# A selective scan on one core: which engine multiplies by C, and a reordering of the small steps around it

## The chip, the cores and the metric

The program runs on one core of one Trainium2 chip. The core has five engines with an instruction queue each: TensorE (PE, with its weight loads PEld), VectorE (DVE), ScalarE (ACT), GpSimd (POOL) and SyncE (SP, which only issues transfers here). Every engine works through its queue in order, and waits on semaphores that others raise. Time is device microseconds (us) from the first to the last instruction. The kernel before took 2139.76 us, the median of three runs (2139.21 to 2142.21).

## The reference, cut to what matters

Sixteen sequences of 256 tokens and 128 features go through four Mamba blocks, a product with Wout, a layer norm, a mixture of eight experts and a second layer norm. One block is:

```python
xn = rmsnorm(x, norm_w)
xp, z = split(xn @ Win, 2)                        # 256 channels each
xc = silu(causal_conv4(xp, conv_w) + conv_b)
dt, Bm, Cm = split(xc @ Wx, [64, 80])             # 64 | 16 | 16
delta = softplus(dt @ Wdt + bdt)
for t in range(256):                              # per sequence, channel, state n of 16
    h = exp(delta[t] * A) * h + (delta[t] * xc[t]) * Bm[t]
    y[t] = sum_n h * Cm[t]
x = x + ((y + xc * Dp) * silu(z)) @ Wblk          # Dp: the skip
```

## The kernel before, in words

The 4096 tokens are eight groups of 512 (two whole sequences). A step is one group in one layer, so there are 32 steps; after them the experts run as a second phase, which the change does not touch. All engines run the same sequence of windows; window s holds the scan of step s, the end of step s-1 and the preparation of step s+1 (and the norm of s+2). Most windows stand in a hardware loop, two per turn.

A window has 16 slots. A slot scans two units of 32 channels x 4 states (128 partitions) over 512 tokens each, so its tile is 128 x 1024. Four slots in a row share an m (0 to 3), the state within a group of four. Per slot:

- **POOL and ACT** (`outer`, L469/L472 and L641) multiply delta * x, with tokens on partitions (`du_t`), by B into `dbu_t`: per m, 8 instructions on POOL and 8 on ACT, in one of two buffers. `POOL_SHARE` and `SHARE` say after which slots they stand, `POOL_FIRST` and `FIRST` the same for m = 0 of the next step.
- **ACT** (`exps`, L563) makes exp(delta * A) in one of four `decay` buffers.
- **PE** (`to_channels`, L1067) turns `dbu_t` by eight transposes into one of two PSUM tiles `dbu_ps`.
- **DVE** (`scan`, L829) runs the recurrence with `decay` (SBUF) and `dbu_ps` (PSUM) into one of eight `ring` tiles (SBUF; the profile's name for it, and for `dbu_t`, is `scan`).
- **DVE** for even slots (`times_c`, L838), **POOL** for odd ones (L478), multiply the ring tile by C (`c_rep`, SBUF) in place.
- **PE** (`quad`, L1052) sums two finished slots over the states into `y_ps`; this frees their ring tiles. DVE's `gate` (L844) multiplies `y_ps` by silu(z) after m = 3.

The preparation of the next step runs between the slots: conv and z projections on PE into the two banks `pre_ps`, Silu on ACT, `project_dbc`, a copy of dt, B and C to `dbc`, `project_dt`, softplus, then `delta`. Softplus is max(v,0) + log(1 + exp(-|v|)): ACT makes |v| (L600) and max(v,0) (L601) for each half, then Exp, Square and Ln; DVE corrects the logarithm in two instructions (L860, L864, both with two SBUF inputs) and adds (L868, `delta`). Sixteen DMAs copy delta to `d_rep` for the next step's exps. POOL forms delta * xc (`du`, L488, in the tile `sp_l`), PE transposes it (`turn_du`, L1145), ACT copies it out (`copy_dut`, L626), and only then can `outer` for m = 0 of the next step begin. `turn_b` and `copy_bt` bring B to token rows, `normalise` (POOL, L450) makes `xn`, `project_out` with `copy_out` ends the previous step, `skip` adds xc * Dp to `y_ps`.

## Time and profile before

| | |
|---|---|
| timed runs | 2139.21, 2139.76, 2142.21 us |
| the profiled execution | span 2143.5 us from first to last instruction; the page has no other time for it |
| before the first scan | 54.4 us |
| the 32 windows | from 54.4 us to 1708.8 us |
| experts | the last 435 us |
| busy share of the span | DVE 91%, PE 88%, ACT 79%, POOL 68% |

Engine shares are over the whole span; in the windows they differ, since POOL has almost nothing to do in the experts. Rows are read so: an engine, the kernel's line, the operation, output and inputs by the program's names, how often, the busy time, the mean duration of one, and the idle time in front with what ended it.

### The profile page before, as it was taken

The numbers are of one execution on the slowest core, as the hardware profiler recorded it, in microseconds if no ns is written. First come the engines' busy times: TensorE is split into PE (matmuls) and PEld (weight loads), VectorE is DVE, ScalarE is ACT, GpSimd is POOL, SyncE is SP. The second block draws the span as 40 slices with busy tenths as digits, with TensorE's granted clock in tenths as the row PEclk, the third lists the DMA queues.
The fourth block names the chain that finished last, engine by engine and source line by source line (L and its number), as shares of the span: only waits on it lengthen the run. The fifth ranks groups of instructions, "written<-read, shape, count | busy, mean of one in ns | idle before, by whom it ended". The sixth has DMA issues, their size and how long they took to land.

```text
span 2143.5 us, 34659 instructions
## 1 busy us (share of the span) xinstructions
PE 1877.8 (88%) x10816; PEld 1183.1 (55%) x10816; DVE 1943.2 (91%) x1826; ACT 1683.8 (79%) x3053; POOL 1458.1 (68%) x1364
## 2 busy tenths in 40 slices
PE   4788888888888888888888888888888799999998
PEld 1444444444444444444444445444444499989998
DVE  3799999999999999999999999999999987767775
ACT  4899999899999998989999999999999433333333
POOL 2688888888888888888888988888889600000000
PEclk9899999999999999999999999999999999999999
DMA  7323232323232323232333333332322200000000
GB/s 241 86 64 79 63 78 62 78 62 78 62 79 63 80 65 79 64 79 65 81 78 73 81 76 79 78 78 62 78 62 72 84 1 11 11 12 11 11 6 11
DMA packets 72786, 138.55 MB, mean 65 GB/s; under 512 B 13072, under 2 KB 31120, under 8 KB 68112
## 3 DMA queue, kind: packets, MB, share of 16 engines
q1 hardware_dynamic: 66320, 119.28, 22.7%
q10 hardware_dynamic: 6400, 18.42, 3.7%
q8 instruction: 39, 0.64, 0.1%
q14 instruction: 27, 0.22, 0.0%
HBM read 63.85 MB, written 7.74 MB: 33 GB/s over the span
## 4 chain that ended last, share of the span: by engine, by line
ACT 27%; PE 26%; POOL 26%; issue 13%; DVE 6%; ACTq 1%; SPq 1%; DMA 1%; POOLq 0%; DVEq 0%
POOL scan L478 12%; POOL scan L472 11%; PE y_ps L1291 11%; ACT decay L563 10%; PE dbu_ps L1266 8%; ACT scan L641 6%; DVE scan L829 3%; POOL scan L469 2%; PE dbu_ps L1067 2%; ACT sp_e L600 2%; ACT delta L601 2%; ACT sp_l L610 2%; PE y_ps L1052 2%; ACT sp_e L605 1%; ACT du_t L626 1%
## 5 line engine op out<-in xcount | busy, mean ns | idle before, releaser
L829 DVE TENSOR_TENSOR_SCAN scan<-decay,dbu_ps 128x1024 f32<-128x1024 f32 x512 | 1154.6, 2274 | 29.8 <-PE dbu_ps L1067 21.9
L1067 PE MATMUL dbu_ps<-ident,scan 128*128 128x128 f32 x4096 | 571.6, 286 | 220.7 <-DVE scan L829 195.9
L478 POOL TENSOR_TENSOR scan<-scan,c_rep 128x1024 f32<-128x1024 f32 x255 | 671.8, 2635 | 130.4 <-ACT du_t L626 66.5
L1067 PEld LDWEIGHTS dbu_ps<-ident,scan 128*128 128x128 f32 x4096 | 482.2, 147 | 500.1 <-DVE scan L829 259.3
L563 ACT ACTIVATE decay<-d_rep,a_cur 128x510 f32<-128x510 f32 x1024 | 668.0, 709 | 54.1 <-POOL scan L478 15.7
L472 POOL TENSOR_SCALAR scan<-du_t,b_t 128x256 f32<-128x256 f32 x896 | 594.8, 679 | 0.0
L641 ACT ACTIVATE scan<-du_t,b_t 128x256 f32<-128x256 f32 x1024 | 445.6, 494 | 1.2
L838 DVE TENSOR_TENSOR scan<-scan,c_rep 128x1024 f32<-128x1024 f32 x257 | 331.0, 1288 | 0.0
L766 ACT ACTIVATE decay<-dbu_ps 128x512 f32<-128x512 f32 x256 | 147.9, 597 | 205.2 <-PE dbu_ps L1266 183.1
L1052 PE MATMUL y_ps<-scan,sel 128*32 128x512 f32 x2048 | 299.8, 661 | 0.0
L1080 PE MATMUL pre_ps<-xn,w_pre 128*128 128x512 f32 x512 | 245.5, 603 | 5.2 <-DVE w_pre L818 5.2
L507 POOL TENSOR_TENSOR sp_e<-sp_e,bout_rep 128x512 f32<-128x512 f32 x8 | 11.2, 1399 | 277.1 <-DMA sp_e<-in_x_rows 277.1
L1266 PE MATMUL dbu_ps<-split_all 128*128 128x512 f32 x768 | 191.3, 400 | 5.8 <-DVE split_all L892 3.5
L1002 DVE TENSOR_TENSOR decay<-decay 128x512 f32<-128x512 f32 x256 | 163.6, 686 | 9.2 <-ACT decay L766 8.1
L1266 PEld LDWEIGHTS dbu_ps<-split_all 128*128 128x128 f32 x768 | 141.1, 190 | 35.2 <-issue 7.7
L989 DVE SCALAR_TENSOR_TENSOR xc<-y_ps,cw,xc 128x128 f32<-128x128 f32 x256 | 72.0, 344 | 95.4 <-PE y_ps L1291 95.4
L1080 PEld LDWEIGHTS pre_ps<-xn,w_pre 128*128 128x128 f32 x512 | 87.8, 191 | 97.4 <-issue 90.6
L488 POOL TENSOR_TENSOR sp_l<-delta,xc 128x1024 f32<-128x1024 f32 x32 | 75.2, 2351 | 81.2 <-DVE delta L868 81.2
L1291 PEld LDWEIGHTS y_ps<-w_pre,decay 128*128 128x128 f32 x1024 | 119.1, 192 | 3.6 <-issue 1.1
L1291 PE MATMUL y_ps<-w_pre,decay 128*128 128x128 f32 x1024 | 119.5, 275 | 0.2 <-DVE decay L1002 0.2
L1291 PEld LDWEIGHTS y_ps<-c_rep,decay 128*128 128x128 f32 x1024 | 118.0, 192 | 1.9
L1291 PE MATMUL y_ps<-c_rep,decay 128*128 128x128 f32 x1024 | 118.1, 275 | 0.0
(110 smaller groups left out, 1648.8 us busy)
## 6 DMA issues: line engine op xcount, KB each, us to landing
d_rep<-delta SPq DMA_DIRECT2D x496, 128.0 KB, 2.9
c_rep<-c_rows SPq DMA_DIRECT2D x32, 1024.0 KB
w_pre<-prepared_weights ACTq DMA_DIRECT2D x15, 866.0 KB, 13.0
prepared_weights<-scan SPq DMA_DIRECT2D x3, 1122.0 KB, 12.9
scan<-in_conv_w SPq DMA_DIRECT2D x4, 512.0 KB, 5.0
w_out<-prepared_weights SPq DMA_DIRECT2D x16, 128.0 KB, 12.5
sp_e<-in_x_rows SPq DMA_DIRECT2D x8, 256.0 KB, 3.2
d_rep<-in_w ACTq DMA_DIRECT2D x2, 1024.0 KB, 6.8
```

The costliest lines, as they stand in the source:

```text
L472: nc.gpsimd.tensor_scalar(dst, src, col, 1.0, ALU.mult, ALU.mult).then_inc(dbut_pool, 1)
L478: nc.gpsimd.tensor_tensor(ring[slot % RING], ring[slot % RING], c_rep[par][:, slot // PRS, :].unsqueeze(1).broadcast_to([128, 2, TG]), ALU ...
L563: last = nc.scalar.activation(decay[slot % DEC][:, u, :, 1:], src[:, :, 1:], ACT.Exp, scale=a_cur[:, b, m:m + 1])
L641: nc.scalar.activation(dbu_t[m % 2][:, j, :, q, :], du_t[par][:, j, :].rearrange("p (b c) -> p b c", b=UNITS), ACT.Copy, scale=b_t[par][:, ...
L829: nc.vector.tensor_tensor_scan(ring[slot % RING].rearrange("p u t -> p (u t)"), decay[slot % DEC].rearrange("p u a t -> p (u a t)"), dbu_p ...
L838: nc.vector.tensor_tensor(ring[slot % RING], ring[slot % RING], c_rep[par][:, slot // PRS, :].unsqueeze(1).broadcast_to([128, 2, TG]), ALU ...
L1002: nc.vector.tensor_tensor(hid[e % 2][:, c, :], hid[e % 2][:, c, :], hid[e % 2][:, c, :], ALU.mult).then_inc(h2_ready, 1)
L1052: last = nc.tensor.matmul(y_ps[k][CH * j:CH * j + CH, :], sel[:, :], ring[slot % RING][:, j % 2, :], start=False, stop=m == M - 1, skip_gr ...
L1067: last = nc.tensor.transpose(dbu_ps[slot % 2][:, u, 128 * j:128 * j + 128], dbu_t[m % 2][:, j, b, :, :].rearrange("p q c -> p (q c)"), ide ...
L1080: tap = nc.tensor.matmul(o, w_pre[:, c0:c0 + 128], xn[:, :, k:k + SEQ], start=k == 0, stop=k == KC - 1, skip_group_check=True)
L1266: last = nc.tensor.matmul(dst, left[l], right[r], start=start and n == 0, stop=stop and n == len(passes) - 1)
L1291: last = nc.tensor.matmul(moe_ps[e % 2][:, DM * j:DM * j + DM], hid[e % 2][:, c, 128 * j:128 * j + 128], w2_sb[e][:, c, :], start=c == 0, ...
```

## The change

Four products by C of a window (slots 0, 5, 12, 14) stay on DVE, and for these slots the scan writes its states back into the PSUM tile that it read, from which the product reads; the other twelve go to POOL. `to_channels` therefore waits for such a product instead of for the scan when it reuses the tile. The bias of delta becomes a row of `w_dt` against a row of ones in `dbc`; ACT takes |v| once over both banks, max(v,0) is no longer stored, and DVE's last sum reads the pre-activation from PSUM (`pre_all`, the two `pre_ps` banks). The order of the small steps and the places of the sums are new; `project_out` goes to `y_ps[1]`.

```diff
+DVE_SLOTS = (0, 5, 12, 14)
+DVE_C = len(DVE_SLOTS)
+POOL_C = SLOTS - DVE_C
-SHARE = (0, 2, 5, 8)
+SHARE = (0, 3, 7, 8)
-POOL_SHARE = (0, 2, 3, 4, 4)
-POOL_FIRST = (0, 0, 2, 3, 4)
+POOL_SHARE = (0, 0, 3, 4, 4)
+POOL_FIRST = (0, 1, 3, 4, 4)
+LOWER_TAPS = (0, 2, 3, 4)
...
+        dbc = sb("dbc", [NBC + 1, TG])
...
-                sp.dma_start(pre[l][:, W_DB:W_DB + KT], bdt[l, :, :]).then_inc(raw_loaded[l], 16)
...
+                sp.wait_ge(dt_cleared, 1)
+                sp.dma_start(pre[l][NBC:NBC + 1, W_DT:W_DT + DI].rearrange("a (k p) -> a k p", k=KT),
+                             bdt[l:l + 1, :, :].rearrange("a p k -> a k p"),
+                             allow_slow_non_contiguous=True).then_inc(raw_loaded[l], 16)
...
-                    elif slot % 2 == 0 and slot and has(s, 0):
+                    elif slot and has(s, 0) and not by_vector(s, slot - 1):
                         times_c(s, i, par, slot - 1)
-                    if slot == 7 and has(s, 2):
+                    if slot == 6 and has(s, 2):
                         normalise(s + 2)
...
+            def softplus_abs(s):
                 wait(act, du_ready, s)
-                for k in range(KT):
-                    act.wait_ge(dt_ready, 2 * s + k + 1)
-                    bias = w_pre[:, W_DB + k:W_DB + k + 1]
-                    bank = pre_ps[1 - k][:, :]
-                    nc.scalar.activation(sp_e[:, k, :], bank, ACT.Abs, bias=bias)
-                    nc.scalar.activation(delta[:, k, :], bank, ACT.Relu, bias=bias).then_inc(dt_used, 1)
+                act.wait_ge(dt_ready, 2 * s + 2)
+                nc.scalar.activation(sp_e[:, :, :], pre_all[:, :, :], ACT.Abs).then_inc(act_sp, 1)
...
+                states = dbu_ps[slot % 2][:, :, :] if by_vector(s, slot) else ring[slot % RING]
+                nc.vector.tensor_tensor_scan(states.rearrange("p u t -> p (u t)"),
...
-                nc.vector.tensor_tensor(ring[slot % RING], ring[slot % RING],
+                nc.vector.tensor_tensor(ring[slot % RING], dbu_ps[slot % 2][:, :, :],
                                         c_rep[par][:, slot // PRS, :].unsqueeze(1).broadcast_to([128, 2, TG]),
                                         ALU.mult).then_inc(hc_dve, 1)
...
-                        if slot % 2:
-                            times_c(s, i, par, slot - 1)
+                        if slot in DVE_SLOTS:
+                            times_c(s, i, par, slot)
...
-                            nc.vector.tensor_tensor(delta[:, :, :], delta[:, :, :], sp_l[:, :, :], ALU.add)\
+                            nc.vector.scalar_tensor_tensor(out=delta[:, :, :], in0=pre_all[:, :, :], scalar=0.0,
+                                                           in1=sp_l[:, :, :], op0=ALU.max, op1=ALU.add)\
...
+                back, before = (s, slot - 2) if slot >= 2 else (s - 1, slot - 2 + SLOTS)
+                if has(s, -1) or slot >= 2:
+                    if by_vector(back, before):
+                        pe.wait_ge(hc_dve, vector_products(back, before))
+                    else:
+                        pe.wait_ge(scan_done, SLOTS * back + before + 1)
```

On POOL, the rows from `du` (L488 before, L507 after) towards the end of the window, in the same early window of both programs. L478 and L497 are products by C; L469 and L472, and after the change L488 and L491, are `outer` (with `du_t1` for this step, with `du_t0` for the next). Before:

```order
L478 TENSOR_TENSOR scan<-scan,c_rep1 128x1024 [waits scan_done]
L472 TENSOR_SCALAR scan<-du_t1,b_t1 128x8x32 x2
L488 TENSOR_TENSOR sp_l<-delta,xc 128x1024 [waits delta_ready]
L472 TENSOR_SCALAR scan<-du_t1,b_t1 128x8x32 x2
...
L478 TENSOR_TENSOR scan<-scan,c_rep1 128x1024 [waits scan_done]
...
L478 TENSOR_TENSOR scan<-scan,c_rep1 128x1024 [waits scan_done]
L469 TENSOR_TENSOR scan<-du_t0,b_t0 128x8x32 [waits bt_ready,dut_ready,dbu_ready]
```

And after:

```order
L497 TENSOR_TENSOR scan<-scan,c_rep1 128x1024 [waits scan_done]
L507 TENSOR_TENSOR sp_l<-delta,xc 128x1024 [waits delta_ready]
L491 TENSOR_SCALAR scan<-du_t1,b_t1 128x8x32 x2
...
L497 TENSOR_TENSOR scan<-scan,c_rep1 128x1024 [waits scan_done]
...
L497 TENSOR_TENSOR scan<-scan,c_rep1 128x1024 [waits scan_done]
...
L488 TENSOR_TENSOR scan<-du_t0,b_t0 128x8x32 [waits bt_ready,dut_ready]
L491 TENSOR_SCALAR scan<-du_t0,b_t0 128x8x32
...
L497 TENSOR_TENSOR scan<-scan,c_rep1 128x1024 [waits scan_done]
L491 TENSOR_SCALAR scan<-du_t0,b_t0 128x8x32 x6
```

The last two `outer` instructions of m = 3 still follow `du`; the two in front of it have gone ahead of a product. The first two of the next step's m = 0 now stand in front of a product (of slot 11), and six behind it.

On PE, the stretch around `to_channels` of slot 12 (into `dbu_ps0`, waiting for `dbut_act` and `dbut_pool`), before; L1145 is `turn_du`, L1052 `quad`:

```order
L1145 MATMUL pre_ps0<-ident,sp_l 128x128 [waits x_ready,bt_ready,du_ready]
...
L1067 MATMUL dbu_ps0<-ident,scan 128x128 [waits scan_done,dbut_act,dbut_pool]
...
L1067 MATMUL dbu_ps1<-ident,scan 128x128 [waits scan_done]
...
L1052 MATMUL y_ps0<-scan,sel 32x512 [waits hc_pool,hc_dve]
```

And after, up to `to_channels` of slot 14; L1161 is `turn_du`, L1073 `quad`, L1106 a conv tap:

```order
L1093 MATMUL dbu_ps0<-ident,scan 128x128 [waits scan_done,dbut_act,dbut_pool]
...
L1161 MATMUL pre_ps<-ident,sp_l 128x128 [waits du_ready]
...
L1093 MATMUL dbu_ps1<-ident,scan 128x128 [waits scan_done]
...
L1073 MATMUL y_ps0<-scan,sel 32x512 [waits hc_pool,hc_dve]
...
L1106 MATMUL pre_ps<-xn,w_pre 128x512 [waits dut_ready,xn_ready]
L1106 MATMUL pre_ps<-xn,w_pre 128x512
L1093 MATMUL dbu_ps0<-ident,scan 128x128 [waits hc_dve]
```

`turn_du` has moved behind `to_channels` of slot 12, two conv taps have come in front of that of slot 14, and the latter now waits for the product of slot 12 (`hc_dve`).

## Rows read from the trace of the kernel before

**Rows 1.** The page: the span, then busy us, share of it and instructions
```profile
span 2143.5 us, 34659 instructions
...
PE 1877.8 (88%) x10816; PEld 1183.1 (55%) x10816; DVE 1943.2 (91%) x1826; ACT 1683.8 (79%) x3053; POOL 1458.1 (68%) x1364
```

**Rows 2.** Busy time of each engine in 1200 us of the windows
```profile
core 0: us, PE busy (x) PEld busy (x) DVE busy (x) ACT busy (x) POOL busy (x), PEclk, DMA share, GB/s
300.00:1500.00 1200.00, 1045.56 (x5688) 571.74 (x5688) 1168.37 (x676) 1103.98 (x1999) 1054.17 (x978) 0.94 0.31 74
```

**Rows 3.** Delta's sum (L868): count, duration ns min/median/max, first and last start
```profile
L868 DVE TENSOR_TENSOR delta<-delta,sp_l x32: 1224/1225/1382, 40.8 to 1635.3; 128x1024 f32<-128x1024 f32 x32
```

**Rows 4.** Groups by line on DVE: busy, mean ns | idle before
```profile
L829 DVE TENSOR_TENSOR_SCAN scan<-decay,dbu_ps 128x1024 f32<-128x1024 f32 x512 | 1154.6, 2274 | 29.8 <-PE dbu_ps L1067 21.9 <-ACT decay L563 4.8
L838 DVE TENSOR_TENSOR scan<-scan,c_rep 128x1024 f32<-128x1024 f32 x257 | 331.0, 1288 | 0.0
L1002 DVE TENSOR_TENSOR decay<-decay 128x512 f32<-128x512 f32 x256 | 163.6, 686 | 9.2 <-ACT decay L766 8.1
L864 DVE SCALAR_TENSOR_TENSOR sp_l<-sp_l,sp_w 128x1024 f32<-128x1024 f32 x32 | 44.0, 1375 | 1.1
L844 DVE TENSOR_TENSOR sz<-sz,y_ps 128x512 f32 (+1 forms) x64 | 42.4, 662 | 0.5 <-PE y_ps L1052 0.5
L860 DVE SCALAR_TENSOR_TENSOR sp_w<-sp_w,sp_e 128x1024 f32<-128x1024 f32 x32 | 40.7, 1272 | 34.8 <-ACT sp_l L610 34.8
```

**Rows 5.** DVE in order of time, two products by C
```profile
786.48 1.26 DVE L838 TENSOR_TENSOR scan<-scan,c_rep 128x1024 f32<-128x1024 f32 x1
...
789.96 0.66 DVE L844 TENSOR_TENSOR sz<-sz,y_ps 128x512 f32 x1
...
792.73 1.20 DVE L838 TENSOR_TENSOR scan<-scan,c_rep 128x1024 f32<-128x1024 f32 x1
```

**Rows 6.** POOL in order of time, the same stretch
```profile
779.15 0.92 POOL L472 TENSOR_SCALAR scan<-du_t,b_t 128x256 f32<-128x256 f32 x2
...
785.28 2.80 POOL L472 TENSOR_SCALAR scan<-du_t,b_t 128x256 f32<-128x256 f32 x4
788.05 2.36 POOL L478 TENSOR_TENSOR scan<-scan,c_rep 128x1024 f32<-128x1024 f32 x1
...
792.90 3.25 POOL L478 TENSOR_TENSOR scan<-scan,c_rep 128x1024 f32<-128x1024 f32 x1 [0.55 <-DVE scan L829]
```

**Rows 7.** Groups by line on POOL
```profile
L478 POOL TENSOR_TENSOR scan<-scan,c_rep 128x1024 f32<-128x1024 f32 x255 | 671.8, 2635 | 130.4 <-ACT du_t L626 66.5 <-DVE scan L829 63.9
L472 POOL TENSOR_SCALAR scan<-du_t,b_t 128x256 f32<-128x256 f32 x896 | 594.8, 679 | 0.0
L469 POOL TENSOR_TENSOR scan<-du_t,b_t 128x256 f32<-128x256 f32 x128 | 78.2, 611 | 15.7 <-PE dbu_ps L1067 11.6 <-ACT du_t L626 4.1
L488 POOL TENSOR_TENSOR sp_l<-delta,xc 128x1024 f32<-128x1024 f32 x32 | 75.2, 2351 | 81.2 <-DVE delta L868 81.2
L450 POOL TENSOR_TENSOR xn<-x,rstd 128x512 f32<-128x512 f32 x32 | 41.2, 1286 | 27.5 <-ACT rstd L547 27.5
```

**Rows 8.** PE in order of time: transposes of a slot, two conv taps, a sum
```profile
780.21 1.09 PE L1067 MATMUL dbu_ps<-ident,scan 128*128 128x128 f32 x8 [0.56 <-POOL scan L472]
...
783.73 1.88 PE L1080 MATMUL pre_ps<-xn,w_pre 128*128 128x512 f32 x4
785.54 1.06 PE L1052 MATMUL y_ps<-scan,sel 128*32 128x512 f32 x8
```

**Rows 9.** PE, the transposes of du in the same window
```profile
818.38 1.56 PE L1145 MATMUL pre_ps<-ident,sp_l 128*128 128x128 f32 x8
```

**Rows 10.** A group by line on ACT: |v| of one half
```profile
L600 ACT ACTIVATE sp_e<-pre_ps,w_pre 128x512 f32<-128x512 f32 x64 | 42.9, 671 | 0.6 <-PE pre_ps L1108 0.6
```

**Rows 11.** The bias's transfer for layer 0: KB, us to landing
```profile
w_pre<-in_bdt SPq DMA_DIRECT2D x1, 1.0 KB, 4.7
```

**Rows 12.** DVE, the first weight product of layer 0 (four instructions)
```profile
12.17 3.45 DVE L811 SCALAR_TENSOR_TENSOR w_pre<-scan,nw 128x256 f32<-128x256 f32 x4 [5.49 <-DMA scan<-in_Wblk]
```

More of the change, by code:

```diff
@@ L304, in is_last, with by_vector, vector_products, pool_products @@
             return has(s, 0) and not has(s, 1)
+        def by_vector(s, slot):
+            return slot in DVE_SLOTS or is_last(s) and slot == SLOTS - 1
+        def vector_products(s, slot):
+            return DVE_C * s + sum(by_vector(s, n) for n in range(slot + 1))
+        def pool_products(s, slot):
+            return POOL_C * s + sum(not by_vector(s, n) for n in range(slot + 1))
         def has(s, offset):
@@ L455, in outer @@
             def outer(s, par, m, first, last):
-                if first == 0:
+                if first == 0 and last:
                     wait(pool, dbu_ready, SLOTS * s + PRS * (m - 1))
@@ L630, in outer @@
             def outer(s, par, m, first, last):
-                if first == 0:
+                if first == 0 and last:
                     wait(act, dbu_ready, SLOTS * s + PRS * (m - 1))
@@ L677, in window @@
                         outer(s, par, 0, FIRST[2], FIRST[3])
+                    if slot == 3 and has(s, 1):
+                        silu_x(s + 1, nxt)
                     if has(s, 0) and m < M and p:
@@ L1192, in window @@
                         project_dbc(s + 1, nxt)
[L1193 removed]
+                    if slot == 6 and has(s, 2):
                         pe.wait_ge(silu_ready, 4 * (s + 2))
                         mean_square(s + 2)
[L1196 to L1201 removed]
@@ L1202, in window @@
-                    if slot == 9 and has(s, -1):
-                        project_out(s - 1, i if par else i - 1, nxt)
+                    if slot == 8 and has(s, -1) and has(s, 0):
+                        project_out(s - 1, i if par else i - 1, nxt)
+                    if slot == 9 and has(s, -1) and not has(s, 0):
+                        project_out(s - 1, i if par else i - 1, nxt)
+                    if slot == 6 and has(s, 1):
+                        turn_b(s + 1)
+                    if slot == 7 and has(s, 1):
+                        project_dt(s + 1, 1)
+                        project_dt(s + 1, 0)
@@ new lines, in window @@
+                    if slot == 9 and has(s, 0):
+                        skip(s, i, par, 1)
+                    if slot == 6 and has(s, 0):
+                        quad(s, 0, 0)
+                    if slot == 9 and has(s, 0):
+                        quad(s, 0, 1)
+                    if slot == 10 and has(s, 0):
+                        quad(s, 1, 0)
+                        quad(s, 1, 1)
+                    if slot in (13, 15) and has(s, 0):
+                        quad(s, 2, slot // 14)
```

169 lines of the change are left out of this document (77 added, 92 removed).

## The prediction, made before the changed kernel ran

> **What bounds the kernel now.** I read the page's busy shares first, then the busy time by engine inside the windows, the groups by line, and last the timelines of DVE and POOL over one stretch.
>
> The page puts DVE first with 91% of the 2143.5 us span [rows 1]; this mixes windows and experts. In 1200 us of windows DVE is busy 1168 us (97%), ACT 1104, POOL 1054, PE 1046 [rows 2]. Delta's sum runs once per step, first at 40.8 and last at 1635.3 us [rows 3]: 31 intervals, so 51.43 us a step. Per step DVE is busy 50.1, ACT 47.3, POOL 45.2 and PE 44.8 us. So DVE bounds the windows; the reader should see how little it idles there: 1.1 us a step before L860, waiting for ACT's logarithm (34.8 us in 31 steps), and 0.9 before the scans [rows 4].
>
> POOL's 45.2 us are not all work. A product by C takes 2.36 us on POOL when DVE runs scans beside it, and 3.25 us when DVE started a product 0.17 us earlier, which then still had 1.03 us to run [rows 5, 6]. Four outer instructions take 2.80 us around DVE's 1.26 us product, against 0.46 each in the undisturbed pair [rows 5, 6]. POOL thus stands still for about 0.86 (0.89/1.03) of the time in which DVE runs an instruction with two SBUF inputs. The means say how much: 8 products at 2.635 instead of 2.36 (2.2 us a step) and 28 outers at 664 ns (594.8 us over 896) instead of 460 (5.7 us) [rows 6, 7]: 7.9 us a step are this wait. Gates have one input in PSUM and do not do it: the one at 789.96 overlaps the end of a POOL product, and neither is longer for it (0.66 and 2.36 us) [rows 5, 6].
>
> **The change part by part.**
>
> *DVE.* Eight products at 1.29 us [rows 4] become four. A product from PSUM has no row; the nearest are the gate, 662 ns for 512 elements with one PSUM input, and L1002, 686 ns with two SBUF inputs [rows 4]. So PSUM costs from 3% less to nothing; I take 1.20, the undisturbed product of [rows 5]. The change takes 8 x 1.29 - 4 x 1.20 = 5.5 us a step off DVE. A scan that writes PSUM has no row either. From below I take nothing gained, as with the gate; from above, one more pass over 1024 elements, 1.20 us, if reading and writing one bank took turns. I take nothing, since a scan at 2.27 us [rows 4] is nearly twice as slow as a product of the same size, so it leaves room. Delta's sum from PSUM stays at 1.23 us [rows 3].
>
> *POOL.* Twelve products x 2.36 = 28.3; 28 outers x 0.46 and 4 x 0.61 (L469) = 15.3; du 2.35; normalise 1.29 [rows 6, 7]: 47.2 us. Two instructions with two SBUF inputs are left on DVE, L860 (1.27) and L864 (1.38) [rows 4]; at 0.86 they cost POOL 2.3 us if it is working then. Sum 49.5 us. POOL becomes the bound, 1.9 us under the present step, provided that it never waits. Now it waits 2.5 us a step for delta (81.2 us in 32) and 2.1 for `du_t` (66.5 in 31) [rows 7], so this needs a walk through the window.
>
> *The walk.* Let POOL start the last product of the old window (slot 15) at 0. Up to du it has 8 products (18.9), 22 outers (10.6) and normalise (1.3): 30.7, with the lock 33.0. DVE from scan 0, if that starts at 0.3: nine scans (20.4), two products (2.4), two gates (1.3), the wait for ACT of 1.1 as now, three delta instructions (3.9): delta at 29.4. POOL arrives 3.6 us later and no longer waits. Behind du it has 2.35 + two outers 0.9 + four products 9.4 + the next m = 0 (3.8) = 16.5: slot 15's product is due at 49.5. Meanwhile the transposes of slot 12 need the two outers behind du (36.3), and take 1.09 [rows 8]: scan 12 starts at 37.4, where DVE alone would have come at 36.2. `turn_du` 1.56 [rows 9], transposes 1.09, a sum 1.06 and two taps 1.88 [rows 8] follow on PE, so slot 14's transposes end at 44.1; DVE could have used them at 43.1 (two scans and a product from 37.4). Then scan 14, product 14, scan 15: 44.1 + 2.27 + 1.20 + 2.27 = 49.9. The product of slot 15 waits 0.4. I add 0.1 for hand-overs that I have not counted: 50.0 us a step.
>
> *Copying du.* With du at 35.4, transposes of slot 12 until 37.4 and `turn_du` until 39.0, ACT's two copies are out soon after 40.1 (11 us of its idle time in all before L626 are too little to matter). POOL reaches the first outer of m = 0 at 41.0. The 2.1 us wait for `du_t` goes, but only about 1 us of room is left.
>
> *ACT.* Four instructions of 671 ns [rows 10] become one over both banks, between 0.67 and 1.34; I take 1.1. ACT falls from 47.3 to 45.7 us, none of it on the path while POOL is the bound: delta could come 3.6 us later.
>
> *PE.* One more row of weights adds no columns; bounded by nothing and one tap (1.88/2, 0.94) [rows 8], I take nothing, since the number of streamed columns is the same. `turn_b` in front of `project_dt` delays |v| by well under the 3.6 us. `project_out` into `y_ps[1]` makes the second skip wait for `copy_out`; it holds the transposes of slot 10 behind it. By the walk these are done about 3 us before scan 10 asks.
>
> *Before the windows.* The bias row lands as 256 single numbers and is now the last transfer of each layer's set. DVE waits 5.49 us for the last of them, until 12.17 [rows 12]; a bias transfer takes 4.7 us to land now [rows 11]. So it costs between nothing and 4.7 us, once; I take 1.5, nearer to nothing, since it is issued in the slot in which the last one was before.
>
> *Sum.* (51.43 - 50.0) x 30 steps = 42.9 us; the first and last windows I leave as they are. Less 1.5: -41.4. From the profiled span of 2143.5 this gives 2102.1. That execution stands 3.7 us above the median of 2139.8, which I carry over: 2098.4, said as 2099.
>
> **A rule against it.** Rows 5 and 6 show the wait between DVE and POOL where DVE has two SBUF inputs, and none beside a gate. The Trainium skill (Perfetto Trace Analysis, Optimizing Scalar/DVE Operations) warns that the two share an SBUF read port, so that moving work from one to the other might not help; by that alone POOL would keep its waits, which is the fourth rival. The Trainium skill (SBUF — State Buffer, Who interferes with whom) narrows it: a DVE instruction with at most one SBUF input, outside the 2-port modes, does not contend. The rows agree with the second, for a gate; no row shows a product from PSUM by C.
>
> **The rivals.**
>
> 1. *POOL gains more.* If the two corrections fall into a time when POOL waits anyway, as now, the lock costs less than 2.3 us and the step falls towards 47.5 to 49; at 48.5 it is -86 us, 2053. For it: today's wait for delta. Against: the walk has POOL busy then.
>
> 2. *The gain goes into waits of queues in order.* Four engines would be busy 45 to 49.5 us of a 50 us step. Places: z's projection holds slot 3's transposes until Silu is through, normalise stands one product earlier and waits for ACT's root, the `du_t` copy has 1 us of room. If these cost 0.6 to 1.5 us a step, the step is 50.6 to 51.5: 2117 to 2144, at 51.2 about 2135. For it: today's 51.43 is itself 1.3 above DVE's busy time. Against: several of these have 1 us or more of cover.
>
> 3. *Slower: the stretch behind du.* Between the transposes of slot 12 and scan 15 nothing gives. Scans 12 and 14 write PSUM, and the tile is free only after the product. If such a scan takes 1.2 us longer, or PE comes that much later with its tile after each of the two, scan 15 ends 2.4 us later, at 52.3; with the 0.1, a step of 52.4: +29 us, +1.5 at the start, 2170 by the median. It decides from 1.5 us of loss per step in this stretch on. For it: PE has 5.6 us of work there for 5.7 us of DVE. Against: the gate shows no price for reading PSUM.
>
> 4. *The products from PSUM still stop POOL.* Four more stops of 0.89 us [rows 6]: 53.6 us a step, +65 us, 2206. Against: the gate.
>
> **How the numbers follow.** The forecast (49.5 to 50.6 us a step, 2084 to 2117) gets 0.50, rival 1 0.10, rival 2 0.25, rival 3 0.12, rival 4 0.03. A change under 0.2% can't be told from none here. Of rival 2 I count 0.17 as faster (under 2135.5) and 0.08 as within 0.2%. So faster 0.77, same 0.08, slower 0.15. The range takes in the upper half of rival 1 and rival 3's cheaper end: 2056 to 2152.
>
> **What would show it.** Right: POOL's products at 2.36 us with almost no spread, POOL busy 48 us or more of a step of 50, its waits for delta and `du_t` nearly gone; DVE idle about 3 us a step, mostly before scans 12 to 14 behind PE; scans into PSUM at 2.27 us and products from it near 1.2. Wrong: POOL idle more than 1 us a step (then another queue bounds, and the row with its wait names it), POOL products still at 3.2 us beside a product from PSUM, or scans of two lengths.

## The result and the profile after

The changed kernel takes 2176.80 us (median of 4 runs, 2175.57 to 2180.03); the kernel before, timed beside it, 2139.85 us (4 runs, 2139.21 to 2142.21). The ratio is 1.0166, 95% interval 1.0147 to 1.0185: slower by 37 us, where 41 us less were forecast, and above the upper end of the range. Runs more than 1.5% above the fastest of the same kernel are left out of the medians, ranges and ratios below: 4631.38 us in experiment 1, 2149.99 us in experiment 4 and 2176.33 us, as long as the changed kernel, in experiment 5.

The page of the changed kernel, against [rows 1]: VectorE (DVE) has 36 us less to do, GpSimd (POOL) 60 us more, and the span is longer all the same.

```profile
span 2175.8 us, 34205 instructions
...
PE 1886.3 (87%) x10816; PEld 1211.2 (56%) x10816; DVE 1907.3 (88%) x1699; ACT 1647.2 (76%) x2957; POOL 1518.0 (70%) x1492
```

The same 1200 us of windows as in [rows 2], and delta's last sum, now L889, as in [rows 3]:

```profile
300.00:1500.00 1200.00, 1027.15 (x5558) 581.60 (x5555) 1127.01 (x572) 1051.76 (x1879) 1068.80 (x1048) 0.94 0.31 71
```

```profile
L889 DVE SCALAR_TENSOR_TENSOR delta<-pre_ps,sp_l x32: 1224/1224/1226, 40.2 to 1666.7; 128x1024 f32<-128x1024 f32 x32
```

(1666.7 - 40.2) / 31 = 52.47 us a step, in place of 51.43. No engine is at its limit in the windows any longer: DVE 94%, POOL 89%. So something waits that was not in the sum, and the groups by line name it (busy us, mean ns | idle before it):

```profile
L497 POOL TENSOR_TENSOR scan<-scan,c_rep 128x1024 f32<-128x1024 f32 x383 | 901.6, 2368 | 77.4 <-DVE scan L849 77.3
L849 DVE TENSOR_TENSOR_SCAN scan<-decay,dbu_ps 128x1024 f32<-128x1024 f32 x383 | 860.0, 2273 | 32.6 <-ACT decay L582 23.7 <-PE dbu_ps L1093 8.5 <-issue 0.2
...
L491 POOL TENSOR_SCALAR scan<-du_t,b_t 128x256 f32<-128x256 f32 x896 | 428.5, 499 | 0.0
L849 DVE TENSOR_TENSOR_SCAN dbu_ps<-decay,dbu_ps 128x1024 f32<-128x1024 f32 x129 | 294.9, 2286 | 36.8 <-PE dbu_ps L1093 36.8
...
L859 DVE TENSOR_TENSOR scan<-dbu_ps,c_rep 128x1024 f32<-128x1024 f32 x129 | 158.0, 1225 | 9.1 <-DMA c_rep<-c_rows 2.5
...
L881 DVE SCALAR_TENSOR_TENSOR sp_w<-sp_w,sp_e 128x1024 f32<-128x1024 f32 x32 | 143.2, 4476 | 49.1 <-ACT sp_l L626 49.1
...
L507 POOL TENSOR_TENSOR sp_l<-delta,xc 128x1024 f32<-128x1024 f32 x32 | 75.0, 2344 | 97.6 <-DVE delta L889 97.6
...
L885 DVE SCALAR_TENSOR_TENSOR sp_l<-sp_l,sp_w 128x1024 f32<-128x1024 f32 x32 | 59.3, 1852 | 1.1
```

Beside [rows 4, 7] the reader is to see two things. POOL's instructions are nearly as short as forecast (products 2.37 us instead of 2.64, outers 0.50 instead of 0.68, with 2.36 and 0.46 forecast), and so are DVE's products from PSUM (1.23) and its scans into PSUM (2.29). But the first correction, L881, an instruction that the change does not touch, has gone from 1.27 us to 4.48, and the second, L885, from 1.38 to 1.85. POOL waits 97.6 us for delta (81.2 before), 3.05 us a step. DVE in order of time in one window (start, duration, [idle before]):

```profile
812.88 4.46 DVE L849 TENSOR_TENSOR_SCAN scan<-decay,dbu_ps 128x1024 f32<-128x1024 f32 x2 [0.48 <-ACT decay L582]
818.65 5.74 DVE L881 SCALAR_TENSOR_TENSOR sp_w<-sp_w,sp_e 128x1024 f32<-128x1024 f32 x1 [1.30 <-ACT sp_l L626]
824.42 1.23 DVE L885 SCALAR_TENSOR_TENSOR sp_l<-sp_l,sp_w 128x1024 f32<-128x1024 f32 x1
825.68 1.23 DVE L889 SCALAR_TENSOR_TENSOR delta<-pre_ps,sp_l 128x1024 f32<-128x1024 f32 x1
```

and POOL in the same window:

```profile
818.05 0.64 POOL L488 TENSOR_TENSOR scan<-du_t,b_t 128x256 f32<-128x256 f32 x1
818.64 2.32 POOL L491 TENSOR_SCALAR scan<-du_t,b_t 128x256 f32<-128x256 f32 x5
820.90 2.40 POOL L497 TENSOR_TENSOR scan<-scan,c_rep 128x1024 f32<-128x1024 f32 x1
826.98 2.34 POOL L507 TENSOR_TENSOR sp_l<-delta,xc 128x1024 f32<-128x1024 f32 x1 [3.68 <-DVE delta L889]
```

L881 is released at 818.65, while an outer runs, and is not let in when that ends (818.69). Five scalings and a whole product of POOL run first, each in its undisturbed time. Only when POOL has nothing left but du, which waits for delta, does L881 run: 823.30 (the product's end) plus 1.1 is its own end. So the two engines wait for each other in turn: DVE 4.5 us for POOL, then POOL 3.7 us for DVE.

The Trainium skill (SBUF — State Buffer, Summary: rules for kernel authors) has the first half of it: a DVE instruction with two SBUF inputs and a GpSimd instruction that reads SBUF exclude each other, and the later one is blocked until the earlier one has finished. The trace shows more than that: here the waiting one is blocked past seven instructions, and five of them had not begun when it was released.

From here on, a table by window says most; it is worked out from the start times of the rows, the mean of windows 2 to 29, us from the start of scan 0. The forecast's line is its walk less 0.3, since scan 0 stood at 0.3 there.

```
                  L881 starts  delta there  du starts  scan 12  scan 14  next scan 0
forecast              25.2        29.1        32.7       37.1     43.8      50.0
changed kernel        25.7        33.9        34.0       40.4     47.0      52.7
```

Until the correction the walk holds to 0.5 us. Then delta is 4.8 us late; as DVE works in order, scan 9 is late by as much, and scan 12 starts 3.3 us late behind DVE's own queue, where POOL should have been what it waits for. From scan 12 to the next window 12.3 us pass (12.9 forecast).

### The profile page after: what moved, and what is told of

Its sections match the earlier page's. It is cut to its first block and busy times, and to the rows that moved or that the text cites. A ratio compares the mean times of both kernels' runs of the same rounds, so it can differ in the third digit from the quotient of the medians.

```text
span 2175.8 us, 34205 instructions
## 1 busy us (share of the span) xinstructions
PE 1886.3 (87%) x10816; PEld 1211.2 (56%) x10816; DVE 1907.3 (88%) x1699; ACT 1647.2 (76%) x2957; POOL 1518.0 (70%) x1492
## 5 line engine op out<-in xcount | busy, mean ns | idle before, releaser
L497 POOL TENSOR_TENSOR scan<-scan,c_rep 128x1024 f32<-128x1024 f32 x383 | 901.6, 2368 | 77.4 <-DVE scan L849 77.3
L849 DVE TENSOR_TENSOR_SCAN scan<-decay,dbu_ps 128x1024 f32<-128x1024 f32 x383 | 860.0, 2273 | 32.6 <-ACT decay L582 23.7
L1093 PEld LDWEIGHTS dbu_ps<-ident,scan 128*128 128x128 f32 x4096 | 505.4, 151 | 520.3 <-DVE scan L849 228.4
L1093 PE MATMUL dbu_ps<-ident,scan 128*128 128x128 f32 x4096 | 601.8, 295 | 197.2 <-DVE scan L849 150.1
L491 POOL TENSOR_SCALAR scan<-du_t,b_t 128x256 f32<-128x256 f32 x896 | 428.5, 499 | 0.0
L849 DVE TENSOR_TENSOR_SCAN dbu_ps<-decay,dbu_ps 128x1024 f32<-128x1024 f32 x129 | 294.9, 2286 | 36.8 <-PE dbu_ps L1093 36.8
L1073 PE MATMUL y_ps<-scan,sel 128*32 128x512 f32 x2048 | 269.8, 611 | 0.0
L1106 PE MATMUL pre_ps<-xn,w_pre 128*128 128x512 f32 x512 | 254.5, 611 | 6.1 <-DVE w_pre L837 5.2
L881 DVE SCALAR_TENSOR_TENSOR sp_w<-sp_w,sp_e 128x1024 f32<-128x1024 f32 x32 | 143.2, 4476 | 49.1 <-ACT sp_l L626 49.1
L859 DVE TENSOR_TENSOR scan<-dbu_ps,c_rep 128x1024 f32<-128x1024 f32 x129 | 158.0, 1225 | 9.1 <-DMA c_rep<-c_rows 2.5
L1106 PEld LDWEIGHTS pre_ps<-xn,w_pre 128*128 128x128 f32 x512 | 86.0, 192 | 110.1 <-issue 101.6
L507 POOL TENSOR_TENSOR sp_l<-delta,xc 128x1024 f32<-128x1024 f32 x32 | 75.0, 2344 | 97.6 <-DVE delta L889 97.6
```

The lines of the kernel that those rows point to most:

```text
L491: nc.gpsimd.tensor_scalar(dst, src, col, 1.0, ALU.mult, ALU.mult).then_inc(dbut_pool, 1)
L497: nc.gpsimd.tensor_tensor(ring[slot % RING], ring[slot % RING], c_rep[par][:, slot // PRS, :].unsqueeze(1).broadcast_to([128, 2, TG]), ALU ...
L849: nc.vector.tensor_tensor_scan(states.rearrange("p u t -> p (u t)"), decay[slot % DEC].rearrange("p u a t -> p (u a t)"), dbu_ps[slot % 2] ...
L859: nc.vector.tensor_tensor(ring[slot % RING], dbu_ps[slot % 2][:, :, :], c_rep[par][:, slot // PRS, :].unsqueeze(1).broadcast_to([128, 2, TG]),
L1073: last = nc.tensor.matmul(y_ps[k][CH * j:CH * j + CH, :], sel[:, :], ring[slot % RING][:, j % 2, :], start=False, stop=m == M - 1, skip_gr ...
L1093: last = nc.tensor.transpose(dbu_ps[slot % 2][:, u, 128 * j:128 * j + 128], dbu_t[m % 2][:, j, b, :, :].rearrange("p q c -> p (q c)"), ide ...
```

## The experiments

The runs of one group share runs of the kernel before on their chip (2141.6 to 2144.0 us median); ratios are to these. Differences to the changed kernel are of medians, from runs on other chips. Line numbers of the same instructions shift by one or two where an edit adds lines.

**1. Is it the kind of instruction?** The first correction as a plain product of two SBUF tiles (its constant is left out, so that the result is not the model's).

```diff
-nc.vector.scalar_tensor_tensor(out=sp_w, in0=sp_w, scalar=LOG_ADD, in1=sp_e, op0=ALU.add, op1=ALU.mult)
+nc.vector.tensor_tensor(sp_w, sp_w, sp_e, ALU.mult)
```

> The changed kernel with the first correction as a plain product of the same two SBUF tiles (LOG_ADD is left out of the computation). If only this kind of instruction (two operations and a scalar) is kept waiting and a plain product is let in at the next end of a POOL instruction, as the products by C were in the kernel before, it takes 1.2 to 1.7 us and the step comes to about 50 us, 2100 us. If the kind does not matter but the run of POOL instructions at its arrival does, it still takes 3 to 6 us in most steps and the time stays at 2165 to 2180 us.

Measured: 2159.12 us (median of 7 runs, 2146.97 to 2172.93), ratio 1.0064 (1.0037 to 1.0092), a little under the 2165 to 2180 expected for this case. The two corrections in its trace:

```profile
L881 DVE TENSOR_TENSOR sp_w<-sp_w,sp_e 128x1024 f32<-128x1024 f32 x32 | 98.4, 3075 | 48.8 <-ACT sp_l L626 48.8
...
L884 DVE SCALAR_TENSOR_TENSOR sp_l<-sp_l,sp_w 128x1024 f32<-128x1024 f32 x32 | 63.6, 1987 | 1.1
```

It is kept waiting too: in windows 2 to 30 it takes 1.4 to 5.8 us, in steps of one POOL instruction. The kind is not the cause; why it is let in somewhat sooner, the run does not tell.

**2. Is it the two SBUF inputs?** Two kernels. In the first each instruction behind the logarithm has one input in PSUM: ScalarE writes its exponential there and max(v, 0) to SBUF; the result is the model's.

```diff
+nc.scalar.activation(delta, pre_all, ACT.Relu)
-nc.scalar.activation(sp_e, sp_e, ACT.Exp, scale=-1.0)
+nc.scalar.activation(pre_all, sp_e, ACT.Exp, scale=-1.0)
 # Square and Ln read pre_all
-nc.vector.scalar_tensor_tensor(out=sp_w, in0=sp_w, scalar=LOG_ADD, in1=sp_e, ...)
-nc.vector.scalar_tensor_tensor(out=sp_l, in0=sp_l, scalar=LN_ERROR, in1=sp_w, ...)
-nc.vector.scalar_tensor_tensor(out=delta, in0=pre_all, scalar=0.0, in1=sp_l, op0=ALU.max, op1=ALU.add)
+nc.vector.scalar_tensor_tensor(out=pre_all, in0=sp_w, scalar=LOG_ADD, in1=pre_all, ...)
+nc.vector.scalar_tensor_tensor(out=pre_all, in0=sp_l, scalar=LN_ERROR, in1=pre_all, ...)
+nc.vector.tensor_tensor(delta, pre_all, delta, ALU.add)
```

> The changed kernel with the whole softplus computed, but so that no instruction of it on DVE has two SBUF inputs: ACT stores max(v,0) in delta (one more ACT instruction of about 1.0 us) and writes Exp back into the two PSUM banks, DVE's corrections keep their running value there, and the last sum takes it from there. Theory 1: corrections at 1.25 us, POOL without stops, step 49.5 to 50.3 us, 2090 to 2115 us, so faster than both kernels. Rival 2 (tile and PE): 2150 to 2177 us. Rival 3 (ACT late): at least 2177 us, since ACT has 1 us more in front of the logarithm.

Measured: 2101.09 us (4 runs, 2095.75 to 2116.53), ratio 0.9807 (0.9756 to 0.9859), faster than both kernels. The wait is gone; the price is DVE's longer wait for the logarithm (74.4 us, 49.1 in the changed kernel), since ScalarE has one instruction more in front of it:

```profile
L491 POOL TENSOR_SCALAR scan<-du_t,b_t 128x256 f32<-128x256 f32 x896 | 415.0, 487 | 0.0
...
L507 POOL TENSOR_TENSOR sp_l<-delta,xc 128x1024 f32<-128x1024 f32 x32 | 76.3, 2385 | 9.2 <-DVE delta L890 9.1
...
L882 DVE SCALAR_TENSOR_TENSOR pre_ps<-sp_w,pre_ps 128x1024 f32<-128x1024 f32 x32 | 39.3, 1229 | 74.4 <-ACT sp_l L627 74.4
L886 DVE SCALAR_TENSOR_TENSOR pre_ps<-sp_l,pre_ps 128x1024 f32<-128x1024 f32 x32 | 39.3, 1228 | 1.1
```

The second leaves ScalarE as it is and exchanges one operand of each correction only.

```diff
-..., in0=sp_w, scalar=LOG_ADD, in1=sp_e, op0=ALU.add, op1=ALU.mult)
+..., in0=pre_all, scalar=0.0, in1=sp_e, op0=ALU.mult, op1=ALU.mult)
-..., in0=sp_l, scalar=LN_ERROR, in1=sp_w, op0=ALU.add, op1=ALU.min)
+..., in0=pre_all, scalar=0.0, in1=sp_w, op0=ALU.mult, op1=ALU.max)
```

> The changed kernel with one operand of each correction replaced: the first reads v from PSUM times 0.0 where it read the square from SBUF, the second the same where it read the logarithm; the logarithm's part of delta is left out of the result. ScalarE does exactly what it did. Theory (VectorE is passed over because both corrections read two tiles of SBUF while GpSimd works back to back): both take 1.2 to 1.3 us without spread, in place of 4.48 and 1.85; delta is 3.5 us earlier, GpSimd hardly waits for it, and the step falls from 52.4 to about 50 us: 2176.8 - 31 x 2.45 = 2101, between 2088 and 2115. Rival (the time goes into ScalarE's new order: logarithm and the long |v| arrive late, and VectorE's 4.48 us hide that): VectorE then idles longer for the logarithm, by 2 to 3 us a step, and the time stays at 2150 to 2180.

Measured: 2113.48 us (6 runs, 2107.30 to 2128.78), ratio 0.9855 (0.9830 to 0.9880).

```profile
L507 POOL TENSOR_TENSOR sp_l<-delta,xc 128x1024 f32<-128x1024 f32 x32 | 76.6, 2394 | 8.3 <-DVE delta L889 8.3
...
L881 DVE SCALAR_TENSOR_TENSOR sp_w<-pre_ps,sp_e 128x1024 f32<-128x1024 f32 x32 | 39.2, 1225 | 48.4 <-ACT sp_l L626 48.4
L885 DVE SCALAR_TENSOR_TENSOR sp_l<-pre_ps,sp_w 128x1024 f32<-128x1024 f32 x32 | 39.2, 1225 | 1.1
```

One operand each, in an instruction of the same kind, length and place, and 63 us are gone: the two SBUF inputs are what the slower kernel pays for. The rival (ScalarE's new order) falls, as DVE's wait for the logarithm did not grow.

**3. Is it that POOL is busy just then?** GpSimd makes du at the head of slot 9, so that it stands idle when the corrections come.

```diff
-if slot == 10 and has(s, 1):
+if slot == 9 and has(s, 1):
     pool.wait_ge(delta_ready, s + 2)
```

> The changed kernel with one order changed: GpSimd makes du at the head of slot 9, ahead of the six outers of m = 3 and the product of slot 8, so that it stands idle, waiting for delta, when the corrections come. Theory (a GpSimd that is busy without a gap keeps VectorE out): the corrections take 1.25 to 1.5 us each, GpSimd waits about 4 us a step for delta (it arrives at 25.4 instead of 33.0 - 2.3, delta is there at 29.4), its step is 47.2 + 4.0 = 51.2 us: 2176.8 - 31 x 1.25 = 2138, between 2110 and 2150. Rival (the corrections are slow whatever GpSimd does, for instance by ScalarE's or PE's traffic): they stay at 3 to 4.5 us, du is no earlier, the outers come later than now, and the time is 2180 to 2260.

Measured: 2190.89 us (5 runs, 2190.09 to 2191.82), ratio 1.0220 (1.0199 to 1.0240). Both corrections take exactly 1225 ns, and POOL waits 4.4 us a step for delta, as expected:

```profile
L507 POOL TENSOR_TENSOR sp_l<-delta,xc 128x1024 f32<-128x1024 f32 x32 | 76.0, 2374 | 141.0 <-DVE delta L889 141.0
...
L881 DVE SCALAR_TENSOR_TENSOR sp_w<-sp_w,sp_e 128x1024 f32<-128x1024 f32 x32 | 39.2, 1225 | 49.1 <-ACT sp_l L626 49.1
L885 DVE SCALAR_TENSOR_TENSOR sp_l<-sp_l,sp_w 128x1024 f32<-128x1024 f32 x32 | 39.2, 1225 | 1.1
```

The theory was right on the wait and its time wrong by 53 us. The eight outers of m = 3, six of which now stand behind du where they stood ahead of it, are what the transposes of slot 12 need; its trace shows PE waiting for them (us, times, longest):

```profile
PE dbu_ps L1093 <- POOL scan L491: 145.8, 33, 5.3
```

Delta is there at 29.5 us, yet scan 12 starts at 40.2, as late as in the changed kernel.

**4. Less for GpSimd.** Six products on VectorE and ten on GpSimd.

```diff
-DVE_SLOTS = (0, 5, 12, 14)
+DVE_SLOTS = (0, 3, 5, 9, 12, 14)
```

> The changed kernel with six products on VectorE (slots 0, 3, 5, 9, 12, 14) and ten on GpSimd, instead of four and twelve: one product less on GpSimd ahead of du and one behind it. Theory (what counts is whether GpSimd is through when the corrections come): GpSimd reaches du at about 30.6 less 2.3 without the lock, delta is due at 30.6, so in most steps the corrections meet an idle GpSimd or its last instruction and take 1.3 to 2.5 us; VectorE has 47.0 us of work and about 3 us of waits behind du: 49.8 to 51 us a step, 2095 to 2135, at 50.3 about 2112. Rival (the loss is one of VectorE's place, not of GpSimd's load): the corrections stay at 4.5 and 1.9 us, VectorE has 2.4 us more a step, 2176.8 + 74 = 2250.

Measured: 2136.22 us (median of 11 runs, 2116.20 to 2147.69), ratio 0.9966 (0.9936 to 0.9996), just above the 2095 to 2135 expected; the profiled run is the shortest of them, with a step of 50.47 us. The corrections:

```profile
L885 DVE SCALAR_TENSOR_TENSOR sp_l<-sp_l,sp_w 128x1024 f32<-128x1024 f32 x32 | 42.4, 1323 | 1.1
L881 DVE SCALAR_TENSOR_TENSOR sp_w<-sp_w,sp_e 128x1024 f32<-128x1024 f32 x32 | 42.2, 1320 | 38.6 <-ACT sp_l L626 38.6
```

They are let in, though not for the reason that I gave: in nearly every window GpSimd is at work when they come, mostly at the same outer as in the changed kernel, and lets them in at its end or one scaling later. So "GpSimd is busy" does not say enough.

**5. What else differs?** In the traces I looked for how long GpSimd had then worked without a gap of 0.1 us (runs from the starts and ends of its rows):

```
kernel, which of the 32   GpSimd without a gap since    first correction takes
before, 1 to 30                  9.7 to 10.1 us              1.22 to 1.48 us
changed, 1                       14.3                        1.75
changed, 2                       25.5                        1.36
changed, 3 to 30                 25.5 to 25.6                2.76 to 5.83
changed, 31                      5.1                         1.28
six products, 1 to 31            5.1 to 5.3                  1.23 to 1.57
```

In the kernel before and with six products POOL waits for a scan some microseconds ahead; in the changed kernel it has fallen so far behind DVE that for these 25.5 us it waits for nothing. One row is against the length alone: window 2 of the changed kernel has the same 25.5 us and is let in at once. I made a gap: GpSimd waits for its own product of slot 6 before it starts that of slot 7. Nothing else changes, and the result is the model's.

```diff
 elif slot and has(s, 0) and not by_vector(s, slot - 1):
+    if slot == 8:
+        pool.wait_ge(hc_pool, pool_products(s, 6))
     times_c(s, i, par, slot - 1)
```

> The changed kernel with one wait more: GpSimd waits for its own product of slot 6 to be finished before it starts that of slot 7, which leaves it idle for some 0.05 to 0.2 us about 3 us before the corrections come; nothing else changes. Theory (a gap, however short, ends the run in which VectorE is passed over): the corrections take 1.25 to 1.6 us, delta is 3 us earlier, the step is 50.0 to 50.6 us: 2176.8 - 31 x 2.2 = 2109, between 2095 and 2130. Rival (the length of the run is a coincidence, or so short a gap does not end it): corrections at 3 to 4.5 us and 2174 to 2184.

Measured: 2143.40 us (median of 9 runs, 2132.59 to 2153.04), ratio 1.0008 (0.9983 to 1.0033): 33 us less than the changed kernel, by one wait more. The corrections take what the theory says; the time stays above its 2095 to 2130, and the step, 51.3 us, above its 50.0 to 50.6 (the part on the prediction says where). The groups:

```profile
L491 POOL TENSOR_SCALAR scan<-du_t,b_t 128x256 f32<-128x256 f32 x896 | 474.0, 548 | 0.0
...
L507 POOL TENSOR_TENSOR sp_l<-delta,xc 128x1024 f32<-128x1024 f32 x32 | 75.7, 2366 | 8.3 <-DVE delta L891 8.3
...
L883 DVE SCALAR_TENSOR_TENSOR sp_w<-sp_w,sp_e 128x1024 f32<-128x1024 f32 x32 | 44.6, 1394 | 49.9 <-ACT sp_l L628 49.9
L887 DVE SCALAR_TENSOR_TENSOR sp_l<-sp_l,sp_w 128x1024 f32<-128x1024 f32 x32 | 44.1, 1379 | 1.1
```

and POOL in one window, with the gap of 0.16 us:

```profile
804.73 2.37 POOL L497 TENSOR_TENSOR scan<-scan,c_rep 128x1024 f32<-128x1024 f32 x1 [0.16 <-POOL scan L497]
807.06 0.61 POOL L488 TENSOR_TENSOR scan<-du_t,b_t 128x256 f32<-128x256 f32 x1
807.65 4.23 POOL L491 TENSOR_SCALAR scan<-du_t,b_t 128x256 f32<-128x256 f32 x5
```

This time DVE's two corrections (from 807.39) stand inside the five scalings, which take 4.23 us in place of 2.32. POOL no longer waits for delta: du follows without a gap.

The edit does not show that it is the gap that counts, as it also moves the moment. In windows 3 to 30 the first correction now finds 0.23 to 0.37 us of the outer still to run; in the changed kernel it found 0.03 to 0.15 (in one window the scaling behind it had just begun). Window 2 of the changed kernel, 25.5 us into a run, found 0.27 us, and was let in when the outer ended:

```profile
139.87 0.60 POOL L488 TENSOR_TENSOR scan<-du_t,b_t 128x256 f32<-128x256 f32 x1
...
140.20 1.36 DVE L881 SCALAR_TENSOR_TENSOR sp_w<-sp_w,sp_e 128x1024 f32<-128x1024 f32 x1 [1.30 <-ACT sp_l L626]
```

The moment alone is not enough either. With six products the correction comes as late, but 5.2 us into a run, and is let in:

```profile
445.63 0.61 POOL L488 TENSOR_TENSOR scan<-du_t,b_t 128x256 f32<-128x256 f32 x1
...
446.21 1.26 DVE L881 SCALAR_TENSOR_TENSOR sp_w<-sp_w,sp_e 128x1024 f32<-128x1024 f32 x1 [0.97 <-ACT sp_l L626]
```

Nor is a late moment always needed: the plain product of experiment 1 was passed over in window 2, 25.3 us into a run, with 0.39 us of the outer left. No run here takes out the gap and keeps the moment.

A second kernel makes the gap later, ahead of the outers of slot 9, by waiting for the logarithm.

```diff
+if slot == 9 and has(s, 1):
+    pool.wait_ge(sp_ready, s + 2)
 if m < M and has(s, 0):
     outer(s, par, m, ...)
```

> The changed kernel with one wait more: GpSimd waits for ScalarE's logarithm ahead of the outers of slot 9. Its product of slot 7 ends 0.85 us after scan 8, the logarithm 1.30 us after it, so this is a gap of about 0.45 us, and the correction and GpSimd's first outer start together. Theory (the gap ends the run): whichever of the two is first, the first correction takes 1.25 to 1.9 us and the second under 1.7; the step is 50.3 to 51: 2176.8 - 31 x 1.8 = 2121, between 2105 and 2140. Rival (GpSimd is simply ahead of VectorE at every boundary): the corrections stay above 3 us, GpSimd loses 0.45 us more: 2177 to 2195.

Measured: 2147.54 us (10 runs, 2137.58 to 2159.94), ratio 1.0025 (1.0004 to 1.0046), above the 2105 to 2140 expected. The first correction, which now finds GpSimd idle, takes 1225 ns in every window, the second 1509 on average; the step is 51.68 us, longer than the 50.3 to 51 expected.

**6. The rule by itself, without the model.** Four programs in which GpSimd runs trains of these instructions and VectorE comes into them with an instruction of the correction's form (the result is a copy of the input). First the two engines alone; then VectorE released by a scan or by ScalarE, without and with load on the other engines; then trains without a gap for up to 31.7 us; then such trains with VectorE's scans, ScalarE, TensorE and transfers beside them.

> Nothing of the reference is computed: only POOL and DVE run, in 40 shots of four kinds, each shot ten times with DVE arriving 50 ns later each time. POOL runs instructions back to back (16 of 256 elements; or 5 products of 1024; or one of 256 after two others as in front of the correction, with a product behind), and DVE asks for one instruction of 1024 with two SBUF inputs, of the kind of the correction or a plain product. If DVE is let in at the end of the POOL instruction that is running, as in the kernel before, the longest DVE row is 1.2 + 0.47 us (1.2 + 2.4 for the long ones). If a run of POOL instructions keeps the port, DVE rows of 5 us and more appear, up to the end of the run, either at all arrival times or at some.

> Not the model: 40 times a train of 16 GpSimd instructions without a gap (two long products, thirteen scalings and one outer product of 256 elements) and in it one VectorE instruction with two SBUF inputs, the correction's form; the output is only copied through. Ten times each: VectorE comes from a scan; it is released by ScalarE, at ten different points of the train; the same with ScalarE going on with eight more instructions; the same with TensorE and a transfer running too. Theory (VectorE is passed over when another engine's signal releases it, or when ScalarE, TensorE and transfers are at work too): in the case that matters VectorE's instruction takes over 2.2 us in more than three of ten, and two or more GpSimd instructions begin inside it. Rival (it needs something else of the full kernel): all 40 are let in at the end of the GpSimd instruction in progress, 1.1 to 1.6 us in a run of scalings, up to 3.5 where a long product is running.

> Not the model: GpSimd works without a gap for one to eight units (a unit is one long product and five scalings, 4.6 us) before a VectorE instruction with two SBUF inputs comes, and for one more unit after it; four times each, then four times eight units with GpSimd waiting for its own last instruction ahead of the last unit; the output is only copied through. In the changed kernel the corrections that were passed over for 2.3 to 5.8 us met a GpSimd that had run 25.5 us without a gap of 0.1 us; those of the kernel before and of the one with six products met one with a gap 5 to 10 us earlier, and were let in at the next boundary. Theory (the length of the run without a gap decides): up to two units (9 us) VectorE is let in at the first boundary, 1.2 to 1.7 us; from five or six units on (23 to 28 us) two or more GpSimd instructions begin inside its instruction, over 2 us; with the wait ahead of the last unit it is let in again. Rival (the length is a coincidence): all 36 take 1.2 to 1.7 us.

> Not the model: GpSimd works 32 us without a gap (seven units of one long product and five scalings), VectorE runs nine scans from PSUM beside it and then, released by ScalarE, one in-place instruction with two SBUF inputs, some 22 us into the run. Six times each: ScalarE idle until then; ScalarE at work all the time; TensorE and transfers too; the same with GpSimd waiting for its own last instruction once, 18 us into the run. The output is only copied through. Open is what, beside the run without a gap, makes GpSimd pass VectorE over, since long runs alone did not. Theory (the load of the other engines or VectorE's own scans during the run): in one of the first three groups two or more GpSimd instructions begin inside VectorE's instruction (over 2 us) in most of the six, and in the fourth it is let in at once (1.2 to 1.7 us). Rival (something else of the full kernel): all 24 take 1.2 to 1.7 us, or up to 3.5 where a long product is running.

Measured: in all 140 cases VectorE is let in when the GpSimd instruction in progress ends, or at the end of the next one at most. It takes 1.16 to 1.61 us, and up to 2.88 only behind a product that had just begun; one row each of the last two programs, the first 31 us and the second 22 us into a train without a gap:

```profile
652.32 1.48 DVE L87 SCALAR_TENSOR_TENSOR dc<-da,db 128x1024 f32<-128x1024 f32 x1 [31.44 <-issue]
```

```profile
483.72 1.48 DVE L144 SCALAR_TENSOR_TENSOR db<-db,da 128x1024 f32<-128x1024 f32 x1 [0.94 <-ACT ab L122]
```

No program shows VectorE passed over, so the theories of the last three fall. A long run without a gap is not enough to bring it about, nor is one with a late moment: one case of the last program came 22.9 us into a train with 0.05 us of the scaling left and took 1.23 us. Where GpSimd waits for its own last instruction in the last two programs, it is idle for 0.08 us only, so they do not test the gap of 0.16 us. What the model has besides stays open.

**7. What bounds the faster kernel?** In the first kernel of experiment 2 windows of 48.2 and 51.9 us alternate (47.2 and 54.6 in the second): every other window brings the next layer's weights. I issued that transfer earlier.

```diff
 if slot == 8 and has(s, 1):
+    if par == 0 and has(s, 2):
+        act.wait_ge(dt_ready, 2 * (s + 1) + 2)
+        load_w_pre(i)
     softplus_abs(s + 1)
     softplus_logs(s + 1)
-    if par == 0 and has(s, 2):
-        act.wait_ge(sp_ready, s + 2)
-        load_w_pre(i)
```

> The kernel e3_lockfree with one transfer issued earlier: the next layer's weights (865 KB, every second step) behind TensorE's last use of the old ones, ahead of |v|, instead of behind the logarithm, some 4 us earlier. In e3_lockfree the steps alternate, 48.1 us and 50 to 55 with the transfer in them; TensorE waited 32.6 us for these weights and ScalarE 46.4 us for the copies of delta, nearly all in the long ones. Theory (the weights come late): the long steps fall to 48.2 to 50, so 2101 - 15 x 2.5 = 2063, between 2045 and 2080. Rival (what is late is the copies of delta, which the transfer slows down wherever it is): no change, 2092 to 2108.

Measured: 2097.78 us (5 runs, 2094.62 to 2099.12), ratio 0.9795 (0.9779 to 0.9810). The rival was right: TensorE no longer waits for the weights, but ScalarE waits longer for the copies of delta (46.4 us without the edit), and the windows come out even, at 49.4 and 49.9. The first correction also starts 1.0 us later than without the edit (27.6 us from scan 0, 26.6 there), so the copies need not be the whole price.

```profile
ACT decay L582 <- DMA d_rep<-delta: 55.0, 20, 6.3
```

## Why the prediction was wrong

The step that failed is the lock's price in the sum for POOL: "Two instructions with two SBUF inputs are left on DVE ... at 0.86 they cost POOL 2.3 us if it is working then." There [rows 5, 6] POOL stands still for DVE, and I took for granted that it is always POOL that does. That holds as long as DVE is let in at once. In the changed kernel, where POOL has by then worked 25.5 us without a gap, it is DVE that stands still, 3.2 us (4.48 - 1.27) and 0.5 us (1.85 - 1.38) a step, ahead of scan 9 in its queue and ahead of delta. The 3.6 us by which POOL should have come later than delta went that way, and POOL waited 3.05 us for delta besides.

The first kernel of experiment 5 puts the forecast's condition back, DVE let in at once and POOL standing still, and shows its numbers in place:

```
                  L881 starts  delta there  du starts  scan 12  scan 14  next scan 0
forecast              25.2        29.1        32.7       37.1     43.8      50.0
with the gap          25.8        29.8        32.6       37.5     45.7      51.3
  odd windows         25.8        29.9        32.6       37.8     44.8      50.5
  even windows        25.8        29.8        32.6       37.2     46.5      52.2
exp. 2, kernel 1      26.6        30.4        30.5       37.5     44.4      50.1
```

The changed kernel misses the forecast by 2.7 us a step (52.7 for 50.0). With the gap 1.4 of them are gone. Of the 1.3 that stay, up to 0.9 are the weights named below, and about 0.5, in all windows, are not traced to a term.

- *DVE.* Eight products less four, 5.5 us: right in size (1.23 for 1.20). Scans into PSUM cost 13 ns more than into SBUF, delta's sum from PSUM nothing.
- *POOL.* Products 2.37 as forecast. The lock by the corrections, where they are let in: L491's 474.0 us less the 412.2 of the kernel of experiment 7 (row below) are 61.8, 2.0 us a step for 2.3 forecast. The size was right for that case; the change did not bring that case about.

```profile
L491 POOL TENSOR_SCALAR scan<-du_t,b_t 128x256 f32<-128x256 f32 x896 | 412.2, 481 | 0.0
```

- *du and scan 12.* With the gap, du starts at 32.6 (32.7 forecast) and scan 12 at 37.5 (37.1). The odd windows come to 50.5 us (50.0).
- *What the walk left out.* In even windows scan 14 waits for PE, which holds its taps for the next layer's weights (33.6 us in 13 waits, below). The transfer is issued behind the logarithm; a shorter window leaves less time for it. In the changed kernel, with its long windows, these waits are under 3 us in all. Half the difference of even and odd windows, 0.9 us a step, is an estimate of its price from above, since in the changed kernel they differ by 1.0 us without such waits. It is a case of rival 2.

```profile
PE pre_ps L1108 <- DMA w_pre<-prepared_weights: 33.6, 13, 4.1
```

- *Rival 3* named 2170 and a step of 52.4, which is nearly what came, by a mechanism that did not: from scan 12 to scan 14 6.6 us pass (6.7 forecast), and scans into PSUM are not longer.
- *Rival 4* was wrong: POOL's products are undisturbed.
- *Before the windows.* Scan 0 starts at 53.78 us (54.35 before): the bias row costs nothing, for 1.5 forecast.
- *What would show it.* "POOL idle more than 1 us a step (then another queue bounds, and the row with its wait names it)": L507 with 97.6 us does. That row leads to L881 in one step.

That experiment 2 ends on the forecast (2101 for 2099) is partly chance: without the lock its odd windows take 48.2, the even ones with the weights 51.9.

What the rows of before could have told: the rule that DVE goes in at once had only been seen with POOL pausing. POOL's 130.4 and 81.2 us of waits [rows 7], which the forecast counted as room to be filled, were what kept its runs short. That DVE went in at once because the runs were short fits experiments 4 and 5, and is not shown.

## What to carry to other kernels

When work goes to the second of two engines that exclude each other, price the exclusion on both: once with the one waiting, once with the other, and take the worse where the waiting instruction stands ahead of the critical chain. An instruction there is best given one operand in PSUM (63 us here, by one operand each), and where that can't be, a wait that makes the other engine pause just ahead is worth a try (33 us here by 0.16 us of pause, though the pause and the moved moment were not told apart). An edit that fills the gaps of an engine can take from others what they used those gaps for; after it, look first at instructions that were not changed and have become longer.
